# Reordering three queues where a run of seven-product blocks begins (single core, fp32 in two halves)

## The chip, the cores and the metric

One NeuronCore of a Trainium2 chip runs the whole program. The metric is the device time of one execution in microseconds (us); the kernel before took a median of 1065.38 us in 3 runs (1064.78 to 1068.34).

## The reference

The input is x, four sequences of 512 rows of 512 features, and two layers follow each other:

```python
q, k, v = x @ Wq, x @ Wk, x @ Wv
a = softmax(q @ k.T * 512**-0.5) @ v @ Wp + bp
cms = gelu(a @ cW1 + cb1) @ cW2 + cb2 + one_hot(code)        # hidden width 2048
mod = gelu(concat([a, cms]) @ mW1 + mb1) @ mW2 + mb2         # hidden width 2048
y = clip(x + cms + mod, 0, 1)
z = y + gelu(y @ W_down[s] + b_down[s]) @ W_up[s] + b_up[s]  # s: expert of the sequence, 3 experts
out = layernorm(z) * ln_w[s] + ln_b[s]
```

Everything is fp32. The kernel makes each fp32 operand into a high half (rounded to the fast matmul format, fp32r) and a low half (the rest), and each product is three matmuls: high x high, high x low, low x high.

## The kernel before

**Tiling.** After attention the kernel walks through 32 groups g. Groups 0 to 15 are the layer cms, groups 16 to 31 (`MOD0` = 16) the layer mod. A group takes 256 hidden columns of one pair of sequences. Its up-projection is a two-by-two block product made with seven products (i = 0 to 6, `product_part`) instead of eight; each has its left operand (a sum of blocks of the weights, `left_x` for the half that multiplies a, `left_c` for the half that multiplies cms) and its right operand (a sum of blocks of the activations). The seven results are joined by VectorE (`join`) into four tiles C11, C22, C21, C12, on which ScalarE applies the gelu (`gelu`), writing H_hi and an fp32 copy; VectorE then makes H_lo (`gelu_low`).

**The down-projection** of group g-1 is done by TensorE inside group g. For the groups in `FOUR` it is the plain `out_tiles`. For the groups in `SEVEN`, which are two runs, `RUNS` = groups 16 to 21 and groups 24 to 30, it is also a seven-product scheme: seven steps j = 0 to 6 (`block_step`), each with two tiles of three matmuls. Steps 0, 1 and 4 take H itself; steps 2, 3, 5 and 6 take the sums T1, T2, T3 and T4 of H (`sum_T` on VectorE, their high half by `T_hi` on ScalarE, their low half by `low_T` on VectorE). The prepared slices of the weights come through four buffers (`ring`), refilled by SyncE in `refill(g-1, j)` after step j has been done. A run begins in group 17 (steps of group 16) and in group 25 (steps of group 24).

**TensorE's order in a group of a run** is fixed: product 0, product 1, steps 0 and 1, product 2, product 3, step 2, product 4, steps 3 and 4, product 5, step 5, product 6, step 6. Step 4 waits until the results of step 2 are added (`add_step`), step 6 until those of step 5 are.

**The other engines** have handwritten orders, each in program order, joined by semaphores:

- SyncE (SP) issues nearly all DMAs: `load_left` (raw columns of the weights, rawX and rawC, 512 KB each), `load_piece` and `save_piece` (24 pieces of the adapter's weights are read, split and stored in memory as high and low halves, one piece a group, groups 3 to 26), `load_staged` (x or cms tiles that are added into acc), `refill`, and in group 24 the saving of the finished `acc` of sequences 0 and 1 and its reloading with x of sequences 2 and 3 (1 MB each, `x_in_acc`).
- GpSimd (POOL) makes the weight sums (`sums_13`, `sum_2`, `sum_4`) and all low halves of left operands (`left_lo`), of pieces (`piece_split`), in group 24 of three operands of cms (`co_lo`, 128x1024), and at the end of y (`y_lo`) and of the last plain second operand (`second_lo`).
- ScalarE (ACT) makes the high halves (`left_hi`, `T_hi`, `piece_to_hi`, `second_hi`) and the gelus. In group g, `left_hi(s, t, 0, g)` waits for the raw columns just loaded, `left_hi` 1, 2 and 4 wait for sums by POOL.
- VectorE (DVE) in a group of a run follows `seven_group`: gelu_low C21, sums V, T3, T4, add_step 0, sum T1, add_step 1, sum T2, low T1, join U2, low T3, T4, T2, add_step 2, join U3 and C22, add_step 3, gelu_low C11, add_staged, add_step 4, join C21, gelu_low C22, add_step 5, join C12, add_step 6.

Of the kernel before, what the change touches and what calls it, by code (L numbers as in the profile page):

```python
# [7 lines left out]
def layers_kernel(nc, x, xT, codes, streams, WqT, WkT, WvT, Wp, bias_cols, cW1, cW2, mW1, mW2,  # L8
# [28 lines left out]
    with ctx:  # L37
# [403 lines left out]
        def _(sp):  # L441
# [30 lines left out]
            def load_left(s, t):  # L472
                if t > 0:
                    sp.wait_ge(A_made[s], 7 * t)
                elif s == 0:
                    sp.wait_ge(WvpT_lo_made, 2 * KT - 1)
                else:
                    sp.wait_ge(out_filled, outputs(MOD0 - 3, 1, 3))
                w = cW1 if s == 0 and t < 8 else mW1[V * s:V * (s + 1), :]
                sp.dma_start(raw[s][:, :, :], w[:, 2 * P * (t % 8):2 * P * (t % 8 + 1)].rearrange("(k p) c -> p k c", p=P)).then_inc(raw_loaded[s], 16)  # L480
# [34 lines left out]
            def refill(g, *steps):  # L515
                for j in steps:
                    if (g, j) in ring_next:
                        sp.wait_ge(out_filled, step(g, j, 1))
                        for load in ring_next[g, j]:
                            load_ring(*load)  # L520
# [6 lines left out]
            def load_piece(u):  # L527
                if u > 0:
                    sp.wait_ge(piece_saved, 32 * u)
                sp.dma_start(piece_raw[:, :], adapter[u // PARTS, u % PARTS]).then_inc(piece_loaded, 16)  # L530

            def save_piece(u):
                e, part = u // PARTS, u % PARTS
                sp.wait_ge(piece_lo_made, u + 1)
                for half, tile in enumerate((piece_hi, piece_lo)):
                    sp.dma_start(experts[e, half, :, 256 * part:256 * (part + 1)], f32(tile[:, :])).then_inc(piece_saved, 16)

            def load_staged(g):
                for i in added_tile(g):
                    if i == 0:  # L540
                        sp.wait_ge(cms_saved[1], 16 * KT)
                    if i > 1:
                        sp.wait_ge(staged_added, i - 1)
                    if g - 1 in SEVEN:
                        sp.wait_ge(out_filled, step(g - 1, 2, 1))
                    elif g - 2 in SEVEN:
                        sp.wait_ge(out_filled, step(g - 2, 6, 1))
                    h, m = i // KT % 2, i % KT
                    src = xT[h, m * P:(m + 1) * P, :] if i < 8 else cms_kept[h, m]
                    sp.dma_start(staged_at(g, i), src).then_inc(staged_loaded[i % 2], 16)  # L550
# [55 lines left out]
            for g in range(MOD0, GROUPS):  # L606
                sets = splits_in(g)
                if g == MOD0:
                    load_left(*sets[0])
                    load_piece(g - 3)  # L610
                    for h in range(2):
                        for m in range(KT):
                            sp.wait_ge(summed, outputs(MOD0 - 1, h, m))
                            sp.dma_start(cms_kept[h, m], acc[:, 2 + h, m, :]).then_inc(cms_saved[h], 16)
                    load_staged(g)
                    fill_ring(g - 1)
                    load_left(*sets[1])
                    save_piece(g - 3)
                    continue
                for s, t in sets:  # L620
                    load_left(s, t)
                if g - 1 not in SEVEN:
                    load_staged(g)
                if g in PIECE_GROUPS:
                    load_piece(g - 3)
                if g - 1 in SEVEN and g < GROUPS - 1:
                    refill(g - 1, 0, 1, 2)
                    load_staged(g)
                    refill(g - 1, 3, 4)
                    if g in FOUR:  # L630
                        load_second(second_set(g))
                    refill(g - 1, 5)
                if g == 23:
                    sp.wait_ge(made, products(g, 0))
                    cms_home(0, B11, B21)
                    sp.wait_ge(made, products(g, 1))
                    cms_home(1, T3, B22)
                    for i in range(2):
                        x1_home(i)
                if g == 24:  # L640
                    sp.wait_ge(clipped, KT)
                    sp.dma_start(y_kept[0], flat(acc[:, 0])).then_inc(y_saved, 16)
                    sp.wait_ge(y_saved, 16)
                    sp.dma_start(acc[:, 0], weight(xT[2])).then_inc(x_in_acc[0], 16)
                if g == GROUPS - 1:
                    sp.wait_ge(made, products(g, 0))
                    sp.dma_start(flat(y01[0][:, :, :]), y_kept[0]).then_inc(y_back[0], 16)
                    sp.wait_ge(made, products(g, 1))
                    sp.dma_start(flat(y01[1][:, :, :]), y_kept[1]).then_inc(y_back[1], 16)
                    sp.wait_ge(piece_saved, 32 * PIECES)  # L650
                    load_adapter(0, (0, 1))
                    refill(g - 1, 0, 1, 2)
                    load_staged(g)
                    sp.wait_ge(made, products(g, 3))
                    load_adapter(0, (2, 3))
                    refill(g - 1, 3)
                    sp.wait_ge(made, products(g, 4))
                    load_adapter(1, range(4))
                    load_second(second_set(g))
                    refill(g - 1, 4, 5)  # L660
                if g in FOUR and g - 1 in FOUR:
                    load_second(second_set(g))
                if g - 1 in FOUR and g in SEVEN:
                    fill_ring(g - 1)
                if g == 24:
                    sp.wait_ge(clipped, 2 * KT)
                    sp.dma_start(y_kept[1], flat(acc[:, 1])).then_inc(y_saved, 16)
                    sp.wait_ge(y_saved, 32)
                    sp.dma_start(acc[:, 1], weight(xT[3])).then_inc(x_in_acc[1], 16)
                if g == 23:  # L670
                    for i in range(2, 7):
                        x1_home(i)
                if g in PIECE_GROUPS:
                    save_piece(g - 3)
                if g - 1 in SEVEN:
                    refill(g - 1, 6)
            sp.wait_ge(made, products(GROUPS - 1, 5))
# [27 lines left out]
        def _(pool):  # L705
# [124 lines left out]
            for g in range(GROUPS):  # L830
                for s, t in splits_in(g - 1) if g > 0 else []:
                    left_lo(s, t, 6)
                    if s == 0 and g - 1 in FOUR and g - 2 in SEVEN:
                        second_lo(second_set(g - 1))
                sets = splits_in(g)
                if g == MOD0:
                    sums_13(*sets[0])
# [54 lines left out]
                    second_lo(second_set(g))  # L892
                for s, t in sets:
                    left_lo(s, t, 5)
                if g in PIECE_GROUPS:
                    piece_split(g - 3)
                if g == GROUPS - 1:
                    for b in range(2):
                        for h in range(2):
                            pool.wait_ge(made, products(g, 2))  # L900
                            pool.wait_ge(y01_hi_made, 2 * b + h + 1)
                            lo(y_lo[b][h][:, :, :], y01[b][:, HALF * h:HALF * (h + 1), :], y_hi[b][h][:, :, :], y01_lo_made)
                if g == GROUPS - 1:
                    second_lo(second_set(g))

            for n in range(POOL_ROWS):
                b, t = n // TT, n % TT
# [251 lines left out]
        def _(act):  # L1159
# [193 lines left out]
            for g in range(GROUPS):  # L1353
# [27 lines left out]
                if g == 1:  # L1381
                    for op in (T3, T4):
                        xo_hi(1, op)
                if g - 1 in SEVEN:
                    T_hi(g - 1, "T1")
                    for s, t in sets[:1]:
                        left_hi(s, t, 0, g)
                    T_hi(g - 1, "T2")
                for i in (0, 1):
                    for s, t in sets[g - 1 in SEVEN and i == 0:]:  # L1390
                        left_hi(s, t, i, g)
                    if g == MOD0 and i == 0:
                        act.wait_ge(cms_saved[1], 16 * KT)
                        for k in (5, 6):
                            left_hi(1, 0, k)
# [5 lines left out]
                    left_hi(1, 0, 0)  # L1401
                for s, t in sets:
                    left_hi(s, t, 2, g)
                gelu(g, C11)
                if g == MOD0:
                    left_hi(*splits_in(g)[1], 0, g)
                if g == 23:
# [26 lines left out]
                if g in PIECE_GROUPS:  # L1434
                    piece_to_hi(g - 3)
            add_b_up(0)
            gelu(GROUPS - 1, C12)
            second_hi(second_set(GROUPS - 1))

            def gelu_adapter(b):  # L1440
                for m in range(BT):
# [476 lines left out]
```

## Time and profile before

| | |
|---|---|
| median of 3 runs | 1065.38 us |
| the profiled execution's own time | 1066.87 us |
| its span, first to last instruction | 1065.1 us |
| mean granted TensorE clock | 0.995 of full speed |
| PE (TensorE matmul) busy | 1051.9 us, 99% |
| DVE, ACT, POOL busy | 68%, 44%, 55% |
| DMA | 37% of 16 engines' span, 125 GB/s |

The times are those of one execution seen by the hardware profiler. Busy time of PE counts matmuls that overlap in the pipeline; how fast they follow each other is seen from their starts. A wait is put down to what was released last; "issue" means that the profile shows nothing.

### The profile page before, as it was taken

Reading aid. Unit: us, or ns where it says so; the run is one execution under the profiler, and the core shown is the slowest. Engines: PE = TensorE matmul, PEld = TensorE weight load, DVE = VectorE, ACT = ScalarE, POOL = GpSimd, SP = SyncE. Lnnn points to the kernel's source line nnn. Section 1 sums busy time; section 2 is a strip of 40 time slices with the busy share of each in tenths; the row PEclk is TensorE's granted clock in tenths of the full one; section 3 lists DMA queues with packets and bytes.
Section 4 is the critical chain, followed back from the end, with each engine's and each line's share of the span. In section 5 each row is a group of like instructions: output and inputs, shape, how many; then the busy total and the mean of one; then the engine's idle time right before and its main releaser. Section 6 shows DMA issues by size and latency. Waiting matters only on the chain. (4 is left out here: it accounts for less than half of the span.)

```text
span 1065.1 us, 13654 instructions
## 1 busy us (share of the span) xinstructions
PE 1051.9 (99%) x4675; PEld 868.9 (82%) x4675; DVE 719.4 (68%) x1020; ACT 473.0 (44%) x901; POOL 586.5 (55%) x577
## 2 busy tenths in 40 slices
PE   9999999999999999999999999999998999999998
PEld 7888888888888888888887888888886888888886
DVE  3735353396565555555786888885797888887868
ACT  3645345454334334333553443443554334343765
POOL 0565774632332331431878767777897666673406
PEclk9999999999999999999999999999999999999999
DMA  7456630101223322111053443435865433345824
GB/s 277 136 171 199 227 109 1 59 1 46 74 74 104 119 74 94 50 35 55 23 176 118 130 125 124 131 107 158 324 220 173 130 122 115 106 117 170 324 80 158
DMA packets 88212, 134.10 MB, mean 126 GB/s; under 512 B 7376, under 2 KB 53200, under 8 KB 87632
## 3 DMA queue, kind: packets, MB, share of 16 engines
q1 hardware_dynamic: 87568, 132.18, 37.2%
q10 hardware_dynamic: 576, 1.05, 0.3%
q8 instruction: 38, 0.62, 0.2%
q14 instruction: 30, 0.25, 0.1%
HBM read 98.34 MB, written 34.87 MB: 125 GB/s over the span
## 5 line engine op out<-in xcount | busy, mean ns | idle before, releaser
L714 POOL TENSOR_TENSOR left_x<-rawX,left_x 128x256 fp32r<-128x256 f32 x144 | 134.5, 935 | 150.9 <-ACT left_x L1202 150.9
L1649 DVE TENSOR_TENSOR acc<-bank,acc 128x512 f32<-128x512 f32 x136 | 92.1, 688 | 50.8 <-PE bank L919 50.3
L1708 DVE TENSOR_TENSOR acc<-bank,acc 128x512 f32<-128x512 f32 x166 | 107.0, 683 | 24.3 <-PE bank L919 22.0
L917 PE MATMUL bank<-H_hi,W_hi 128*128 128x512 f32 x304 | 118.4, 390 | 0.4 <-POOL W_lo L714 0.4
L918 PE MATMUL bank<-H_lo,W_hi 128*128 128x512 f32 x304 | 118.3, 389 | 0.0
L919 PE MATMUL bank<-H_hi,W_lo 128*128 128x512 f32 x304 | 118.3, 389 | 0.0
L917 PE MATMUL bank<-x_T_hi,left_x 128*128 128x512 f32 x256 | 99.8, 390 | 0.0
L918 PE MATMUL bank<-x_T_lo,left_x 128*128 128x512 f32 x256 | 99.8, 390 | 0.0
L919 PE MATMUL bank<-x_T_hi,left_x 128*128 128x512 f32 x256 | 99.6, 389 | 0.0
L1638 DVE TENSOR_TENSOR u_t<-bank,s_t 128x512 f32<-128x512 f32 x64 | 44.0, 688 | 75.7 <-PE bank L919 73.6
L714 POOL TENSOR_TENSOR left_c<-rawC,left_c 128x256 fp32r<-128x256 f32 x96 | 91.2, 950 | 3.8 <-ACT left_c L1202 3.8
L1202 ACT ACTIVATE left_x<-rawX 128x256 fp32r<-128x256 f32 x144 | 57.7, 408 | 63.9 <-POOL rawX L728 44.6
L714 POOL TENSOR_TENSOR piece_lo<-piece_raw,piece_hi 128x256 fp32r<-128x256 f32 x24 | 20.1, 839 | 106.0 <-ACT piece_hi L1331 106.0
L917 PE MATMUL bank<-x_B_hi,left_x 128*128 128x512 f32 x192 | 74.9, 390 | 0.0
L918 PE MATMUL bank<-x_B_lo,left_x 128*128 128x512 f32 x192 | 74.9, 390 | 0.0
L919 PE MATMUL bank<-x_B_hi,left_x 128*128 128x512 f32 x192 | 74.8, 390 | 0.0
L1315 ACT ACTIVATE H_hi<-u_t,bias 128x512 fp32r<-128x512 f32 x51 | 36.6, 717 | 86.0 <-PE bank L919 83.3
L1315 ACT ACTIVATE H_hi<-bank,bias 128x512 fp32r<-128x512 f32 x32 | 22.0, 687 | 111.0 <-PE bank L919 111.0
L917 PEld LDWEIGHTS bank<-H_hi,W_hi 128*128 128x128 f32 x304 | 57.0, 188 | 12.8 <-POOL W_lo L714 1.1
L919 PEld LDWEIGHTS bank<-H_hi,W_lo 128*128 128x128 f32 x304 | 57.1, 188 | 12.0
L918 PEld LDWEIGHTS bank<-H_lo,W_hi 128*128 128x128 f32 x304 | 57.1, 188 | 11.7
L917 PE MATMUL bank<-H_hi,ring 128*128 128x512 f32 x156 | 61.3, 393 | 2.6 <-issue 2.6
(224 smaller groups left out, 2825.7 us busy)
## 6 DMA issues: line engine op xcount, KB each, us to landing
ring<-w_kept SPq DMA_DIRECT2D x91, 256.0 KB, 2.7
rawX<-mW_dram SPq DMA_DIRECT2D x16, 512.0 KB, 4.1
rawC<-mW_dram SPq DMA_DIRECT2D x16, 512.0 KB, 4.8
w_kept<-mod_hi SPq DMA_DIRECT2D x7, 896.0 KB, 4.4
w_kept<-mod_lo SPq DMA_DIRECT2D x7, 896.0 KB, 7.2
xT_raw<-xT_dram SPq DMA_DIRECT2D x4, 1024.0 KB, 8.1
x_raw<-x_dram SPq DMA_DIRECT2D x4, 1024.0 KB, 6.3
rawX<-cW_dram SPq DMA_DIRECT2D x8, 512.0 KB, 3.7
```

Source lines behind the costliest of these rows:

```text
L714: pool.tensor_tensor(dst, src, f32(hi), ALU.subtract).then_inc(done, 1)
L917: pe.matmul(tile, sh, mh, start=first_one and n == 0, stop=False, skip_group_check=joined_group)
L918: pe.matmul(tile, sh, ml, start=False, stop=False, skip_group_check=joined_group)
L919: last = pe.matmul(tile, sl, mh, start=False, stop=last_one and n == len(terms) - 1, skip_group_check=joined_group)
L1202: act.activation(left(s, i)[0], left_source(s, i), ACT.Copy).then_inc(A_hi_made[s], 1)
L1315: act.activation(dst, src, ACT.Gelu, bias=bias[:, column:column + 1]).then_inc(gelu_made, 1)
L1638: dve.tensor_tensor(dst[:, :], bank[b][:, :], other[:, :], ALU.add).then_inc(joined, 1)
L1649: op = dve.tensor_tensor(dst, src, dst, ALU.add)
L1708: dve.tensor_tensor(dst, src, dst, ALU.add).then_inc(summed, 1)
```

## The change

All edits are orders; no operation is added or left out.

- ScalarE, groups 17 and 25 (`run_starts`): high half of T2 ahead of left operand 0 of x, and gelu of C11 directly behind left operands 0, ahead of 1 and 2.
- SyncE: a piece is stored in the next group, behind `load_left`, and the next one is loaded behind the staged tiles (in group 24 behind the ring's first slices); group 16 no longer ends with a save. x of sequence 3 is loaded into `acc` in group 25, behind the raw columns and the piece's save.
- GpSimd, groups from 17 on: a piece is split in the next group, behind left operands 6. At the end `second_lo` goes ahead of the last of four y_lo.
- ScalarE, end of group 31: `second_hi` ahead of the gelu of C12.

```diff
@@ SyncE, groups from 16 on
                     fill_ring(g - 1)
                     load_left(*sets[1])
-                    save_piece(g - 3)
                     continue
                 for s, t in sets:
                     load_left(s, t)
+                if g - 1 in PIECE_GROUPS:
+                    save_piece(g - 4)
                 if g - 1 not in SEVEN:
                     load_staged(g)
-                if g in PIECE_GROUPS:
-                    load_piece(g - 3)
                 if g - 1 in SEVEN and g < GROUPS - 1:
+                    if g == 25:
+                        sp.wait_ge(y_saved, 32)
+                        sp.dma_start(acc[:, 1], weight(xT[3])).then_inc(x_in_acc[1], 16)
                     refill(g - 1, 0, 1, 2)
                     load_staged(g)
+                    if g in PIECE_GROUPS:
+                        load_piece(g - 3)
                     refill(g - 1, 3, 4)
...
                     for i in range(2):
                         x1_home(i)
+                    load_piece(g - 3)
...
                 if g == 24:
+                    load_piece(g - 3)
                     sp.wait_ge(clipped, 2 * KT)
                     sp.dma_start(y_kept[1], flat(acc[:, 1])).then_inc(y_saved, 16)
-                    sp.wait_ge(y_saved, 32)
-                    sp.dma_start(acc[:, 1], weight(xT[3])).then_inc(x_in_acc[1], 16)
...
-                if g in PIECE_GROUPS:
-                    save_piece(g - 3)
                 if g - 1 in SEVEN:
                     refill(g - 1, 6)
@@ GpSimd
                     left_lo(s, t, 6)
                     if s == 0 and g - 1 in FOUR and g - 2 in SEVEN:
                         second_lo(second_set(g - 1))
+                if g > MOD0 and g - 1 in PIECE_GROUPS:
+                    piece_split(g - 4)
...
-                if g in PIECE_GROUPS:
+                if g < MOD0 and g in PIECE_GROUPS:
                     piece_split(g - 3)
                 if g == GROUPS - 1:
                     for b in range(2):
                         for h in range(2):
+                            if b == 1 and h == 1:
+                                second_lo(second_set(g))
                             pool.wait_ge(made, products(g, 2))
...
-                if g == GROUPS - 1:
-                    second_lo(second_set(g))
@@ ScalarE
+                run_starts = g - 1 in (RUNS[0][0], RUNS[1][0])
                 if g - 1 in SEVEN:
                     T_hi(g - 1, "T1")
-                    for s, t in sets[:1]:
+                    for s, t in sets[:0 if run_starts else 1]:
                         left_hi(s, t, 0, g)
                     T_hi(g - 1, "T2")
                 for i in (0, 1):
-                    for s, t in sets[g - 1 in SEVEN and i == 0:]:
+                    for s, t in sets[g - 1 in SEVEN and i == 0 and not run_starts:]:
                         left_hi(s, t, i, g)
+                    if run_starts and i == 0:
+                        gelu(g, C11)
...
                 for s, t in sets:
                     left_hi(s, t, 2, g)
-                gelu(g, C11)
+                if not run_starts:
+                    gelu(g, C11)
...
             add_b_up(0)
+            second_hi(second_set(GROUPS - 1))
             gelu(GROUPS - 1, C12)
-            second_hi(second_set(GROUPS - 1))
```

## Rows read from the trace of the kernel before

**Rows 1.** The waits of PE over the whole span: us in total, times, longest.

```profile
PE bank L917 <- DVE acc L1708: 3.4, 2, 3.1
PE bank L917 <- issue: 2.6, 2, 2.2
```

**Rows 2.** PE by stretches: length, busy (matmuls), clock granted, DMA share, GB/s.

```profile
573.20:588.82 15.62, 13.07 (x49) 0.89 0.44 152
606.50:617.39 10.89, 10.89 (x49) 1.00 0.32 84
809.20:828.45 19.25, 15.78 (x61) 0.91 0.39 126
```

**Rows 3.** The same view, a shorter stretch.

```profile
823.00:826.20 3.20, 3.20 (x9) 0.50 0.06 18
```

**Rows 4.** PE in order of time: start, duration, line, op, [idle before <- releaser].

```profile
575.63 0.47 PE L917 MATMUL bank<-H_hi,ring 128*128 128x512 f32 x1 [2.25 <-issue]
...
776.60 0.39 PE L917 MATMUL bank<-c_B_hi,left_c 128*128 128x512 f32 x1
...
809.78 0.47 PE L917 MATMUL bank<-H_hi,ring 128*128 128x512 f32 x1 [0.39 <-issue]
...
822.67 0.58 PE L917 MATMUL bank<-T_hi,ring 128*128 128x512 f32 x1 [3.08 <-DVE acc L1708]
...
1003.13 0.50 PE L917 MATMUL bank<-H_hi,W_hi 128*128 128x512 f32 x1 [0.43 <-POOL W_lo L714]
```

**Rows 5.** ACT in order of time, groups 17, 24 and 31.

```profile
573.59 0.42 ACT L1202 ACTIVATE left_x<-rawX 128x256 fp32r<-128x256 f32 x1 [7.43 <-DMA rawX<-mW_dram]
573.91 0.61 ACT L1319 ACTIVATE H_hi<-H_f 128x512 fp32r<-128x512 f32 x1
...
794.21 0.40 ACT L1331 ACTIVATE piece_hi<-piece_raw 128x256 fp32r<-128x256 f32 x1
...
999.55 1.06 ACT L1209 ACTIVATE W_hi<-W_raw 128x1024 fp32r<-128x1024 f32 x1 [0.51 <-DMA W_raw<-mW_dram]
```

**Rows 6.** The page's group of ACT's gelu of C11: xcount | busy, mean ns | idle.

```profile
L1315 ACT ACTIVATE H_hi<-bank,bias 128x512 fp32r<-128x512 f32 x32 | 22.0, 687 | 111.0 <-PE bank L919 111.0
```

**Rows 7.** DVE in order of time, groups 17 and 25.

```profile
574.56 0.97 DVE L1690 TENSOR_TENSOR H_lo<-H_f,H_hi 128x512 fp32r<-128x512 f32 x1 [5.06 <-ACT H_hi L1319]
...
801.84 0.68 DVE L1690 TENSOR_TENSOR H_lo<-H_f,H_hi 128x512 fp32r<-128x512 f32 x1
...
816.08 1.02 DVE L1624 TENSOR_TENSOR H_lo<-gelu_f,H_hi 128x512 fp32r<-128x512 f32 x1 [2.37 <-ACT gelu_f L1315]
...
821.84 1.28 DVE L1708 TENSOR_TENSOR acc<-bank,acc 128x512 f32<-128x512 f32 x2
```

**Rows 8.** POOL in order of time, groups 16 to 17, then 24.

```profile
566.58 1.19 POOL L714 TENSOR_TENSOR piece_lo<-piece_raw,piece_hi 128x256 fp32r<-128x256 f32 x1
...
568.92 1.18 POOL L714 TENSOR_TENSOR left_c<-rawC,left_c 128x256 fp32r<-128x256 f32 x1
...
770.84 3.39 POOL L714 TENSOR_TENSOR c_B_lo<-c_B_f,c_B_hi 128x1024 fp32r<-128x1024 f32 x1
...
798.76 0.74 POOL L714 TENSOR_TENSOR left_x<-rawX,left_x 128x256 fp32r<-128x256 f32 x1
```

**Rows 9.** SyncE's DMA issues in order of time.

```profile
571.87 1.38 SPq L513 DMA_DIRECT2D ring<-w_kept  x3
...
799.54 0.38 SPq L669 DMA_DIRECT2D acc<-xT_dram  x1
```

**Rows 10.** DMA issues: KB each, median us to landing; page, 569.5 to 574, 799 to 802.

```profile
ring<-w_kept SPq DMA_DIRECT2D x91, 256.0 KB, 2.7
...
ring<-w_kept SPq DMA_DIRECT2D x3, 256.0 KB, 4.4
...
acc<-xT_dram SPq DMA_DIRECT2D x1, 1024.0 KB, 5.9
rawC<-mW_dram SPq DMA_DIRECT2D x1, 512.0 KB, 7.6
```

## The prediction

> **What bounds the kernel now.** The page's first part, in the table above, has PE busy for 99% of the span, so nothing is gained but by closing PE's own gaps. The list of PE's waits is the next view: over the whole span it stands for 3.4 us on adds by VectorE and 2.6 us on "issue" [rows 1], and little else. Then PE by stretches. From step 3 of group 18 to its end TensorE is undisturbed: 48 matmuls (the view's 49 counts one cut by the edge) in 10.89 us, 0.227 us each, at the full clock. The same 48 matmuls in group 17 take 15.62 us; in group 25 the same work and the 12 matmuls of the next product take 19.25 us where 60/48 x 10.89 = 13.61 would do [rows 2]. So the start of the first run loses 15.62 - 10.89 = 4.73 us, that of the second 19.25 - 13.61 = 5.64 us, together 10.37 us. That is more than the waits, because the granted clock falls too: 0.89 and 0.91 as means of the stretches, 0.50 (1.2 GHz of 2.4) inside the second, right behind its stop [rows 2, 3]. About 1.6 us of each loss is this half clock: 3.4 us of it at half speed, from 1.00 - 0.89 = 0.11 of 15.62 us taken twice.
>
> PE in order of time gives the places [rows 4]. I call a product 12 x 0.227 = 2.72 us and a step 6 x 0.227 = 1.36 us.
> - 575.63, group 17, step 3, after 2.25 us of idle: its operand is T2.
> - 809.78, group 25, step 3 again, 0.39 us.
> - 822.67, group 25, step 6, 3.08 us, for the adds of step 5.
> - 1003.13, the last group's plain tiles, 0.43 us, for POOL's W_lo.
>
> **Why T2 is late.** ACT stood 7.43 us before left operand 0 at 573.59, for the raw columns; T2's high half came only behind it, at 573.91, and VectorE, which had been idle for 5.06 us, made the low half from 574.56 to 575.53 [rows 5, 7]. PE went on at 575.63. T2's sum is ahead of all that in VectorE's order, so T2 was ready for ACT before 569.50, when VectorE's idle time began.
>
> **Why the adds of step 5 are late.** VectorE's chain from gelu_low of C11 is gelu_low, staged adds, add_step 4, join C21, gelu_low C22, add_step 5. In group 25 it begins at 816.08, after 2.37 us of waiting for ACT's gelu, and its first add of step 5 ends at 821.84 + 0.64 = 822.48: 6.4 us [rows 7]. The gelu itself stands in ACT's order behind left operands 2, whose sums POOL starts only when the raw columns are there.
>
> **Edit 1, T2 first (ACT).** In group 17 its high half is made before 569.5, its low half by 569.50 + 0.97 = 570.5; PE asks at 573.2. In group 25, where VectorE's T1 low half was at 801.84 [rows 7], three more operations of 0.6 us separate it from T2's: about 804.9 against 809.2. Both stops at step 3 go. Next in line is step 4.
>
> **Edit 2, C11's gelu early (ACT).** It still needs the results of step 3. In group 25 PE does that from 809.2 to 810.6; +0.15 for the pipeline, two activations of 0.69 us [rows 6] give 812.1, and the chain's 6.4 us give 818.5. PE, running through, reaches step 6 at 809.2 + 3 x 1.36 + 2 x 2.72 = 818.7. So it just fits, by 0.2 us, and I keep 0 to 0.8 us of stop, taking 0.2. In group 17 the chain has one staged tile instead of two and about 1.2 us more of room. ACT now stands before the gelu with left operands 1 behind it. POOL waits for those until about 812.4 in group 25, but PE wants them in group 26, at 820.1 + 2.7 = 822.8: nothing is lost.
>
> The 6.4 us hold one size that can move. Low halves on VectorE take 0.68 us at 801.84 and 1.02 us at 816.08 for the same shape [rows 7]. The Trainium skill's page "SBUF — State Buffer", section Who interferes with whom, says that a VectorE instruction with two SBUF inputs and a GpSimd instruction that reads SBUF share a port pair, and the later one blocks. By that rule the chain would be up to 1 us shorter if POOL stood still while it ran, and the 0.2 us would go; but POOL, released by left operands 1, runs again from 812.4, so I leave the chain as measured.
>
> **Edit 3, pieces split and stored behind left 6 (POOL, SP), group 17.** Before, POOL split the piece at 566.58 for 1.19 us ahead of left 6, whose second half ran 568.92 to 570.10 [rows 8]. Now the left operands end at about 567.8 and 568.9, so the raw loads go 1.2 to 1.9 us earlier; the split ends at 570.1 as before. SP then issues two stores (an issue costs 0.46 us, from 1.38 for 3 [rows 9]) and the ring's slices for steps 4, 5 and 6 at 571.0, against 571.87. Loading the next piece, with its wait, is out of the way. Slice 4 is wanted at 573.2 + 1.36 = 574.6. A ring load takes 2.7 us as the median of 91 and 4.4 us in this very place, behind the raw columns and the piece [rows 10]: landing at 573.7 to 575.4. The raw loads are now 2 to 3 us ahead of it, not 1.7, so I take 574.4: no stop, but up to 0.8 us stays in the range; I take 0.2. In the later groups of the runs SP waits for the split before it asks for slices 4 to 6. These have cover: from the end of step 0, when slice 4 may be asked for, to step 4 there are 2 x 1.36 + 1.36 + 3 x 2.72 = 12.2 us, less 2.7 for the load. The piece load behind the staged tiles has 5 us or more there; nothing for either.
>
> **Edit 4, x of sequence 3 in group 25 (SP).** It was issued at 799.54 and took 5.9 us [rows 9, 10]; rawX and rawC stood behind it, and rawC took 7.6 us. Now they go first, which is what feeds POOL and ACT. The price is that the add of step 2 gets its x later. POOL's left 6 was at 798.76 [rows 8]. It gains 1.2 us by the split behind it and loses 0.7 to 1.7 us by the previous piece's split, which now stands in front of the three `co_lo` of group 24, so its second half ends at about 800.5 and the split at 801.5. Two stores, then x at 802.5 to 803.3; +5.9 gives 808.4 to 809.2, +7.6 (behind the raw columns) 810.1 to 810.9. Step 4 starts at 810.6 and waits for the first add of step 2, 0.64 us: x must be there by 809.9. I take 808.8, so nothing, and keep 0 to 1 us. The first `co_lo`, moved by 0.7 to 1.7 us, ended at 770.84 + 3.39 = 774.23 and PE needs it at 776.60 [rows 4, 8]: covered; beyond 2.4 us it would cost one for one.
>
> The page "DMA: Bandwidth & Descriptors" of the Trainium skill, section Queues, rings and completion order, says that each engine takes the descriptors of one issuing queue in ring order. Taken strictly, x would wait for every byte of the raw columns, which is the 7.6 us end, and the sum would be about 0.6 us smaller; the trace's 4.4 against 2.7 us for a ring slice agrees.
>
> **Edit 5, piece 21 behind the ring's slices in group 24 (SP).** ACT took it at 794.21 [rows 5]. It is now issued around 789.6, ahead only of the saving of sequence 1, whose landing released SP at 799.54 [rows 9]; that save is 1 MB, some 3 us of transfer, so the piece lands at 796 to 797.5. ACT, and with it C12's gelu, T3, the adds and T1, come 2 to 3.3 us later. T1's low half ended at 802.52 and PE asks at 809.2 - 2.72 - 1.36 = 805.1: room for 2.6 us. 0 to 0.8 us; I take 0.2.
>
> **Edit 6, second_lo and second_hi at the end.** ACT began W_hi at 999.55, released by the DMA, and POOL's W_lo followed it at once: neither stood behind what it is moved past [rows 4, 5]. Worth nothing; the 0.43 us stay. C12's gelu and the last y_lo, 2 to 2.5 us later, are used after a further 5.4 us of matmuls.
>
> **Sum.** 10.37 us less 0.2 (step 6), 0.2 (slice 4), 0.2 (T1) = 9.8 us. 1066.87 - 9.8 = 1057.1 us for an execution like the profiled one; the median is 1.49 us below that one, so 1055.6 us.
>
> **Rivals.**
> - *x arrives late.* Step 4 of group 25 stands for the add of step 2. It decides if x lands after 809.9; the row of rawC speaks for it, the one of x itself against. A stop of 1 us shifts the whole chain to step 6 as well, which has 0.2 us; with the half clock (1.6 us) 2.6 to 3.5 us come back: 1058.5 us. Chance 0.15.
> - *Slice 4 arrives late in group 17.* 0.8 us, and the clock perhaps falls again: 2.4 us back, 1058.0 us. Against it: the two short stops of 0.39 and 0.43 us [rows 4] had no fall of the clock behind them. 0.12.
> - *The second chain doesn't close.* ACT's gelu of C11 waits for something else, or POOL slows VectorE: the 3.08 us of step 6 shrink to 1.5 only and the clock still falls, so 1.5 + 1.6 = 3.1 us come back: 1058.7 us; if the first start fails in the same way, 1061.8 us. 0.10.
> - *Slower.* SP is one queue, and in each of the nine groups of the runs that have a piece to store it now waits for POOL's split before it fetches slices 4 to 6. This decides once POOL's left 6 and split end more than 9.5 us (12.2 - 2.7) after step 0; PE arrives some 5 us earlier at groups 18 and 26 than before, POOL only 2 to 3 us. If it bites by 1 us with the half clock in most of them, 8 x 2.6 = 21 us are added and 9.8 gained: 1077 us. PE has no wait at all in groups 18 to 22 now (the list [rows 1] is of the whole span), and POOL's 55% leave it time to catch up. 0.03.
>
> The forecast has 0.60. **Range:** the low end is the sum with no residue and a median 1 us luckier, 1053.8 us; the high end takes in the first three rivals' usual size, 1060.3 us. A change within 0.3% (3.2 us, about what a measurement of this kernel can tell from none) would need two thirds of the gain to fail. Faster 0.91, same 0.06, slower 0.03.
>
> **What would show it.** Right: PE's list without "issue"; step 3 of groups 17 and 25 joined to product 4; ACT's T2 near 569 and 804; gelu of C11 at 574.7 and 810.8; the stretches of rows 2 near 10.9 and 13.6 us with clock 1.00; W_lo's 0.4 us still there. Wrong: a stop before step 4 in either group, released by the ring or by an add of step 2; T1 late in group 25; a half clock without a long stop; a wait of SP for the split that reaches PE.

## The result, and the profile after

| | before | after |
|---|---|---|
| median, 6 runs each | 1067.2 us | 1061.5 us (1059.8 to 1062.52) |
| ratio, 95% interval | | 0.9944 [0.9929, 0.9959] |
| profiled span | 1065.1 us | 1060.7 us |
| PE's stops from 210 us on, sum | 11.0 us | 6.95 us |

Faster, by 5.7 us of 1067.2, where 9.8 was forecast; 1061.5 us lies above the range of 1053.8 to 1060.3. The three runs on which the forecast's level rested were 1.8 us faster than the median of six (1065.38 against 1067.2), which would put the forecast at 1057.4 us. The other 4.1 us are gain that did not come. The profiled execution after took 1062.52 us and is the slowest of its six, so its stops may be about 1 us more than those of a middle one.

"Stops" here and below: two matmuls in a row start 0.227 us apart at full speed, and what a pair has beyond that is lost. It is read from the starts in PE's order of time and is 0.1 to 0.2 us more than the idle time printed there. Each stop at full clock costs a further 0.08 to 0.11 us one matmul later. At half clock the excess of every matmul counts.

PE's list of waits of the kernel after (us in total, times, longest), to set beside [rows 1]:

```profile
PE bank L921 <- DVE acc L1716: 1.8, 2, 1.0
PE bank L947 <- POOL ident L712: 1.5, 1, 1.5
PE bank L921 <- DMA ring<-w_kept: 1.4, 1, 1.4
PE bank L921 <- POOL W_lo L716: 1.4, 1, 1.4
PE bank L921 <- issue: 0.7, 1, 0.7
```

The longest stop is 1.4 us instead of 3.1, but there are five of them. (POOL's ident is at the start of the program and is in every kernel.) The stretches of [rows 2], from step 3 to the end of step 6, with the next product in the second:

```profile
572.78:586.36 13.58, 11.45 (x50) 8.85 (x48) 10.21 (x14) 7.95 (x19) 12.06 (x16) 1.00 0.51 166
808.04:823.12 15.08, 14.05 (x62) 11.11 (x60) 14.43 (x20) 8.55 (x20) 13.84 (x17) 1.00 0.43 142
```

The columns are length, busy (count) of PE, weight loads, VectorE, ScalarE and GpSimd, then clock, DMA share, GB/s. Group 17 went from 15.62 to 13.58 us where 10.89 was wanted, group 25 from 19.25 to 15.08 where 13.61 was. The clock is 1.00 in both: the half clock is gone. PE in order of time gives the five places:

```profile
575.67 0.50 PE L921 MATMUL bank<-H_hi,ring 128*128 128x512 f32 x1 [1.37 <-DMA ring<-w_kept]
...
584.89 0.47 PE L921 MATMUL bank<-T_hi,ring 128*128 128x512 f32 x1 [0.77 <-DVE acc L1716]
...
803.86 0.47 PE L921 MATMUL bank<-H_hi,ring 128*128 128x512 f32 x1 [0.75 <-issue]
...
818.91 0.47 PE L921 MATMUL bank<-T_hi,ring 128*128 128x512 f32 x1 [1.03 <-DVE acc L1716]
...
998.71 0.50 PE L921 MATMUL bank<-H_hi,W_hi 128*128 128x512 f32 x1 [1.35 <-POOL W_lo L716]
```

They are step 4 of group 17 (1.53 us by the starts), its step 6 (0.93), step 2 of group 25 (0.91), its step 6 (1.19) and the last group's plain tiles (1.51). None is at step 3, where T2 held PE before. The mean granted clock is 0.999 or 1.0 in all six executions, so it was not this one alone that lost the half clock. Each has its own cause, and the other engines' order of time shows it.

**Step 4 of group 17: slice 4.** SyncE's issues, and the issues with their median time to landing:

```profile
567.34 0.38 SPq L480 DMA_DIRECT2D rawX<-mW_dram  x1
568.54 0.84 SPq L480 DMA_DIRECT2D rawC<-mW_dram  x1
...
570.57 1.47 SPq L513 DMA_DIRECT2D ring<-w_kept  x3
```
```profile
ring<-w_kept SPq DMA_DIRECT2D x3, 256.0 KB, 5.2
rawX<-mW_dram SPq DMA_DIRECT2D x1, 512.0 KB, 3.9
rawC<-mW_dram SPq DMA_DIRECT2D x1, 512.0 KB, 5.7
```

Everything was asked for earlier than before (slice 4 at 570.57 against 571.87 [rows 9]) and took longer (5.2 us against 4.4 [rows 10]): slice 4 came at 575.62, wanted at 574.1. By the semaphore's events in the trace it came in 16 parts, from 574.14 to 575.62, and PE went on behind the last of them, at 575.67; in the kernel before they came from 575.69 to 576.06. The spread of 1.5 us is about as long as the stop. Fifteen parts were there by 575.09; why the last one lagged no run shows.

**Step 6 of group 17: the gelu of C22.** ScalarE and VectorE:

```profile
575.20 0.68 ACT L1319 ACTIVATE gelu_f<-bank,bias 128x512 f32<-128x512 f32 x1
...
579.49 0.42 ACT L1206 ACTIVATE left_c<-rawC 128x256 fp32r<-128x256 f32 x1 [1.43 <-POOL rawC L730]
...
581.66 0.71 ACT L1319 ACTIVATE H_hi<-u_t,bias 128x512 fp32r<-128x512 f32 x1
...
583.01 1.13 DVE L1632 TENSOR_TENSOR H_lo<-u_t,H_hi 128x512 fp32r<-128x512 f32 x1 [2.24 <-ACT u_t L1319]
584.07 1.27 DVE L1716 TENSOR_TENSOR acc<-bank,acc 128x512 f32<-128x512 f32 x2
```

Left operand 1 of the half that multiplies cms (left_c) waits for a sum by POOL that was ready at 579.4. Seven high halves, this one included, go before the gelu of C22 in ScalarE's order, the low half of C22 behind that gelu, and the adds of step 5 behind the low half. PE had stood at this step in the kernel before too, for 0.31 us (0.47 by the starts), the second of the two waits in [rows 1]:

```profile
587.36 0.47 PE L917 MATMUL bank<-T_hi,ring 128*128 128x512 f32 x1 [0.31 <-DVE acc L1708]
```

**Step 2 of group 25: piece 21.** ACT stood for the piece until 796.00, and T1's low half started at 802.54:

```profile
796.00 0.42 ACT L1335 ACTIVATE piece_hi<-piece_raw 128x256 fp32r<-128x256 f32 x1 [4.17 <-DMA piece_raw<-adapter_dram]
```
```profile
802.54 1.22 DVE L1698 TENSOR_TENSOR H_lo<-H_f,H_hi 128x512 fp32r<-128x512 f32 x1
```

**Step 6 of group 25: x.** VectorE, and the DMA issues of 800 to 802.6:

```profile
808.55 1.41 DVE L1714 SCALAR_TENSOR_TENSOR acc<-bank,bias,acc 128x512 f32<-128x512 f32 x2 [1.85 <-DMA acc<-xT_dram]
...
812.59 0.74 DVE L1632 TENSOR_TENSOR H_lo<-gelu_f,H_hi 128x512 fp32r<-128x512 f32 x1
```
```profile
acc<-xT_dram SPq DMA_DIRECT2D x1, 1024.0 KB, 7.3
```

C11's gelu was done at 810.95 (two activations from 809.68), its low half began only at 812.59. In between VectorE did what the late x had held up: the add of step 2, two joins, the add of step 3. That is 1.6 us, and the stop at step 6 is 1.19.

**The end: W_raw.** ScalarE and GpSimd in group 31:

```profile
995.15 1.06 ACT L1213 ACTIVATE W_hi<-W_raw 128x1024 fp32r<-128x1024 f32 x1 [2.67 <-DMA W_raw<-mW_dram]
```
```profile
996.29 2.37 POOL L716 TENSOR_TENSOR W_lo<-W_raw,W_hi 128x1024 fp32r<-128x1024 f32 x1 [3.69 <-ACT W_hi L1213]
```

W_raw took 9.9 us to land, and both of its users stood waiting for it.

### The profile page after: what moved, and what is told of

It is laid out like the page before. It is cut to its first block, busy times and chain, and to the rows that moved or that the text cites. A ratio compares the mean times of both kernels' runs of the same rounds, so it can differ in the third digit from the quotient of the medians.

```text
span 1060.7 us, 13654 instructions
## 1 busy us (share of the span) xinstructions
PE 1048.7 (99%) x4675; PEld 866.4 (82%) x4675; DVE 721.6 (68%) x1020; ACT 473.5 (45%) x901; POOL 591.9 (56%) x577
## 4 chain that ended last, share of the span: by engine, by line
PE 87%; POOL 4%; DVE 3%; DMA 3%; issue 2%; ACT 1%; SPq 0%; DVEq 0%; ACTq 0%; POOLq 0%
PE bank L921 28%; PE bank L923 28%; PE bank L922 28%; POOL left_c L716 1%; POOL left_x L716 1%; DMA piece_raw<-adapter_dram 1%; DVE c_T_f L1580 1%; DMA acc<-xT_dram 1%; PE bank L978 1%; PE bank L1144 1%; DVE acc L1657 0%; DVE acc L1724 0%; DMA ring<-w_kept 0%; POOL rawC L730 0%; DVE H_lo L1632 0%
## 5 line engine op out<-in xcount | busy, mean ns | idle before, releaser
L716 POOL TENSOR_TENSOR piece_lo<-piece_raw,piece_hi 128x256 fp32r<-128x256 f32 x24 | 23.8, 992 | 106.1 <-ACT piece_hi L1335 106.1
```

What stands on the lines that cost most here:

```text
L716: pool.tensor_tensor(dst, src, f32(hi), ALU.subtract).then_inc(done, 1)
```

## Experiments

Theory A reads the five stops as above: ScalarE's order (the third sum behind left operands 1) and four transfers. The ratio is to runs of the kernel before on the same chip, whose median was 1067.15 us (15 runs) for ring17, piece21, end_undone and act_only, 1067.6 (17) for c22, w_raw, sp_pool_only and best, and 1066.38 (7) for x_back and act_c22_wraw. Stops are given in the order step 4 and step 6 of group 17, step 2 and step 6 of group 25, W_lo; the sum holds the small ones too. The kernel after: 1.53, 0.93, 0.91, 1.19, 1.51, sum 6.95 us. Stops are those of one profiled execution, the times medians of 4 to 10.

**ring17: slices 4 and 5 ahead of the raw columns in group 17.**

```diff
+                if g in (17,):
+                    refill(g - 1, 0, 1)
                 for s, t in sets:
                     load_left(s, t)
...
-                    refill(g - 1, 0, 1, 2)
+                    refill(g - 1, *((2,) if g in (17,) else (0, 1, 2)))
```

> The changed kernel with one more move: in group 17 SyncE asks for the ring's slices for steps 4 and 5 ahead of the raw columns, in an idle stretch. Theory A (landings): the stop of 1.53 us ahead of step 4 is slice 4 standing in the DMA queue behind 1 MB of raw columns and a piece, so it goes, and PE waits there for nothing; the time falls by 1 to 1.6 us against the changed kernel, ratio to before about 0.993. The stop of 0.9 us before step 6 of group 17 stays or grows by up to 1 us, for the gelu of C22 hangs on rawC, which still lands near 574.2. Theory B (order of the engines: ACT's gelu of C11 ahead of left operands 1 makes the stops): slice 4 is only the first in line, PE stops at step 4 or 5 for a result of VectorE and the sum of the two stops, 2.5 us, stays.

Measured 1062.41 us, 0.9963 [0.995, 0.9976], span 1060.0. Stops: none, 2.04, 1.30, 1.34, 0.98, sum 6.07. The stop of slice 4 is gone and that of step 6 has grown by 1.11 us: they are in series, and the second is set by ScalarE and GpSimd, who did not move:

```profile
581.47 0.71 ACT L1321 ACTIVATE H_hi<-u_t,bias 128x512 fp32r<-128x512 f32 x1
```

581.47 against 581.66. By the interval this is no better than the kernel after: the removal of one stop in a series was worth nothing. Four of the ten executions have a mean granted clock of 0.996 to 0.998 and are the four slowest (1063.48 to 1066.29 us); the other six, at 0.999 or 1.0, took 1060.68 to 1062.98 us, about what the kernel after takes. With a stop of about 2 us the clock seems to fall in some executions and not in others; the profiled one is of the second kind, and where it fell in the four no trace shows.

**c22: C22's gelu ahead of left operands 1 as well.**

```diff
                     if run_starts and i == 0:
                         gelu(g, C11)
+                        gelu(g, C22)
...
-                gelu(g, C22)
+                if not run_starts:
+                    gelu(g, C22)
```

> The changed kernel with the gelu of C22 also ahead of left operands 1 in groups 17 and 25. In the changed kernel ACT stood before left operand 1 of c until 579.5, for POOL's third sum, and the gelu of C22 came at 581.7, its low half at 583.0. Theory A (that place in ACT's order makes the stop before step 6 of group 17): it goes, 0.9 us. In group 25 the stop of 1.2 us stays, for there VectorE is late by x of sequence 3. Time 1 us under the changed kernel. Theory B (the staged tile, which landed at 577.6, sets it): the stop stays at 0.5 us or more.

Measured 1060.31 us, 0.9924 [0.9895, 0.9953]. Stops: 1.80, none, 1.41, 1.16, 1.43, sum 6.61. The stop of group 17's step 6 is gone, that of group 25 is not (x holds it), and ScalarE shows why:

```profile
577.67 0.72 ACT L1319 ACTIVATE H_hi<-u_t,bias 128x512 fp32r<-128x512 f32 x1 [1.54 <-PE bank L923]
```

The gelu now waits for PE itself and is 4 us earlier.

**piece21: the piece loaded behind the save of piece 20**, at the head of group 24's loads, instead of behind the ring's slices.

```diff
                 if g - 1 in PIECE_GROUPS:
                     save_piece(g - 4)
+                if g == 24:
+                    load_piece(g - 3)
...
                 if g == 24:
-                    load_piece(g - 3)
                     sp.wait_ge(clipped, 2 * KT)
```

> The changed kernel with piece 21 loaded behind the store of piece 20 again, ahead of the saving of y in group 24, so that it is there long before ACT asks. Theory A: ACT's idle time of 4.2 us in front of it goes, T1's low half is 2 us earlier, PE's stops of 0.14 and 0.91 us before product 3 and step 2 of group 25 go. POOL's left 6 and the raw columns are then 2 us earlier too, and x of sequence 3 with them, so the 1.2 us before step 6 shrink to 0.5 or less. Time 1 to 2 us under the changed kernel. Theory B: T1 stays late because the adds of VectorE are what it waits for; stop of about 0.9 us stays before step 2, and the time is the same.

Measured 1060.43 us, 0.9947 [0.993, 0.9964], span 1057.7. Stops: 0.50, 0.80, none, 1.11, 1.41, sum 4.52. Step 2's stop is gone, alone of the five. The stop at step 6 was expected to shrink to 0.5 us or less, and did not: x landed 2.8 us earlier, at 805.60, but PE was 2.8 us earlier too. That of slice 4 shrank as well, by 1.0 us, with nothing changed in group 17; more on that below.

**x_back: edit 4 alone undone**, x asked for in group 24 again, ahead of the raw columns.

```diff
-                    if g == 25:
-                        sp.wait_ge(y_saved, 32)
-                        sp.dma_start(acc[:, 1], weight(xT[3])).then_inc(x_in_acc[1], 16)
...
                     sp.dma_start(y_kept[1], flat(acc[:, 1])).then_inc(y_saved, 16)
+                    sp.wait_ge(y_saved, 32)
+                    sp.dma_start(acc[:, 1], weight(xT[3])).then_inc(x_in_acc[1], 16)
```

> The changed kernel with edit 4 alone undone: x of sequence 3 is asked for behind the saving of sequence 1 in group 24 again, ahead of the raw columns of group 25. Theory A (the stop of 1.19 us at step 6 of group 25 is x's landing at 808.43, which holds VectorE's add of step 2 and all behind it): x lands by 804, gelu_low of C11 starts within 0.2 us of its gelu, and the stop at step 6 shrinks to 0.6 or less; the raw columns land 1 to 2 us later without a stop of their own; step 4 of group 17, step 6 of group 17, step 2 of group 25 and W_lo keep 0.9 to 1.9 us each. Median 1060.3 to 1061.2 us. Rival B (the raw columns' later landing moves the stop: gelu of C22 waits behind left operands 1 instead, as in the run with ScalarE's edits alone): the stop at step 6 keeps 0.9 to 1.3 us and the time stays at 1061.5. Rival C (x did not matter): as after in every stop.

Measured 1058.88 us, 0.9928 [0.99, 0.9956], span 1057.1. Stops: 1.03, 0.71, 0.36 (with 0.30 two products earlier), none, 0.95, sum 3.90. x and the raw columns, by issue and landing:

```profile
797.48 0.38 SPq L672 DMA_DIRECT2D acc<-xT_dram  x1
```
```profile
acc<-xT_dram SPq DMA_DIRECT2D x1, 1024.0 KB, 5.6
rawX<-mW_dram SPq DMA_DIRECT2D x1, 512.0 KB, 6.7
rawC<-mW_dram SPq DMA_DIRECT2D x1, 512.0 KB, 7.6
```

x came at 803.1 instead of 808.4 and the stop at step 6 went; rawC came at 806.1 instead of 805.0; ScalarE stood 1.16 us for it, PE did not. Edit 4 cost its own stop, 1.2 us. Rival B fell: C22's gelu stood behind left operands 1, at 813.13, in time. Step 2 of group 25 and step 6 of group 17 were expected to keep 0.9 us or more and came out at 0.36 and 0.71; nothing in their orders had moved.

**w_raw: the second operand's load ahead of the adapter's in group 31.**

```diff
-                    load_adapter(1, range(4))
                     load_second(second_set(g))
+                    load_adapter(1, range(4))
```

> The changed kernel with the last raw operand W_raw asked for ahead of the four 512 KB loads of adapter 1, after step 4. Theory A (the 1.5 us stop before the last plain tiles is its landing, behind 2 MB in the queue): it lands 4 us earlier or more, W_lo is made before the 24 matmuls with y are over, and the stop is gone: 1.5 us under the changed kernel. Only now the moved second_lo is worth something. Theory B (ACT's or POOL's place for it): the stop stays near 1 us.

Measured 1060.71 us, 0.9925 [0.9899, 0.9951], span 1057.9. Stops: 0.61, 0.83, 1.39, 1.33, none, sum 4.78. W_raw took 5.9 us instead of 9.9 and the last stop is gone.

**end_undone: edit 6 alone undone** (`second_lo` behind the fourth y_lo, `second_hi` behind the gelu of C12).

```diff
-                            if b == 1 and h == 1:
-                                second_lo(second_set(g))
...
+                if g == GROUPS - 1:
+                    second_lo(second_set(g))
...
-            second_hi(second_set(GROUPS - 1))
             gelu(GROUPS - 1, C12)
+            second_hi(second_set(GROUPS - 1))
```

> The changed kernel with the end of group 31 as before: second_hi behind the gelu of C12 and second_lo behind all four y_lo. Theory A: the stop before the last plain tiles, 1.5 us against 0.6 before, is the landing of W_raw (9.9 us instead of 8.5), so it stays at 0.6 to 1.5 us and the time is that of the changed kernel within 0.5 us. Theory B: the two moved operations lengthen it, and it is back at 0.6 us.

Measured 1062.19 us, 0.9956 [0.994, 0.9973]. Stops: 1.42, 0.47, 1.23 (and 0.48), 1.34, 1.86, sum 7.43. GpSimd began W_lo at 996.22, after 1.71 us of waiting for W_hi, against 996.29 with edit 6. Edit 6 moves nothing while W_raw is late. The stop of 1.86 us lies above the 0.6 to 1.5 that were expected: W_raw took 10.2 us.

**act_only: the kernel before with ScalarE's edits of groups 17 and 25, and no others.** The diff is that of ScalarE's queue without its last hunk.

> The kernel before with the edit on ScalarE alone (T2 and gelu of C11 ahead in groups 17 and 25), nothing of SyncE and POOL moved. Theory A: it is the larger part of the gain. Group 17: the stop at step 3 goes, but slice 4 was asked for at 571.87 and lands at 576.1, so PE stops 1.5 us before step 4 in its place. Group 25: step 3's 0.4 us go; slice 4 is issued at 806.6 and lands at 810.2, in time; x of sequence 3 is in time, gelu of C11 starts at 810.8, but rawC lands at 809.2 and left 1 and the gelu of C22 wait for POOL's third sum, so step 6 stops 1 to 2 us instead of 3.1. About 4 to 5 us gained, ratio 0.9955. Theory B: the order on ScalarE alone gives most of the changed kernel's remaining stops and no more than 2 us.

Measured 1061.0 us (1060.64 to 1061.47), 0.995 [0.9933, 0.9966], span 1058.8. Stops: 1.00, 1.25, none, 1.08, 1.18, sum 5.02. That is the gain of the whole change: on top of these two edits, all the others together move neither median nor interval. Slice 4 cost 1.0 us of the 1.5 expected; the 1.25 us at step 6 of group 17 were not expected. At step 6 of group 25 x is in time (5.9 us to landing, from 797.36), and the trace has C22's gelu behind left operands 1 there too (act_c22_wraw below tests it):

```profile
812.22 0.42 ACT L1202 ACTIVATE left_c<-rawC 128x256 fp32r<-128x256 f32 x1 [1.87 <-POOL rawC L728]
...
814.39 0.71 ACT L1315 ACTIVATE H_hi<-u_t,bias 128x512 fp32r<-128x512 f32 x1
```

**sp_pool_only: the change without these edits of ScalarE.**

```diff
-                run_starts = g - 1 in (RUNS[0][0], RUNS[1][0])
+                run_starts = False
```

> The changed kernel without its edits on ScalarE in groups 17 and 25: only SyncE's, POOL's and the end's moves are left. Theory A (the edits on ScalarE give the gain, those on SyncE and POOL only move transfers): T2 waits again for rawX, which now lands 1.9 us earlier in group 17 and 5 us earlier in group 25, so step 3 stops about 0.5 us in group 17 and not at all in 25; step 4 stops 1 to 1.5 us for slice 4; gelu of C11 is late again, and step 6 stops 0.5 us in group 17 and up to 2 us in 25; T1 of group 25 is late by piece 21 as in the changed kernel. About 2 to 4 us gained on the kernel before, ratio 0.997. Theory B (the raw columns' earlier loading is what gains): 0.995 as the changed kernel, and ScalarE's edits add nothing to it.

Measured 1064.07 us, 0.9959 [0.9942, 0.9977], span 1063.9. Stops: 0.58, 2.29, 1.28, 1.30, 1.33, and 0.69 at step 3 of group 17, 0.35 at product 3 of group 25; with a half clock the sum is 10.2. So the moves of SyncE and GpSimd do gain by themselves, 3.5 us between the medians, but at the same stops as ScalarE's: step 3 of group 17 went from 2.41 to 0.69 and step 6 of group 25 from 3.24 to 1.30 us. The two gains overlap and don't add. Loading the raw columns earlier does bring T2's high half forward, to 571.83 from 573.91 [rows 5]. The stop at step 6 of group 17 grew from 0.47 us to 2.29, and behind it the clock fell. This profiled execution, 1065.69 us, is the slowest of ten (the fastest took 1062.29), so its sum stands high.

```profile
586.22 0.47 PE L921 MATMUL bank<-T_hi,ring 128*128 128x512 f32 x1 [2.13 <-DVE acc L1716]
```
```profile
586.60:590.00 3.40, 3.40 (x10) 2.62 (x9) 2.60 (x5) 1.89 (x5) 3.08 (x6) 0.50 0.03 8
```

**act_c22_wraw: the kernel before with ScalarE's edits of groups 17 and 25, c22 and w_raw**, and none of the moves of SyncE and GpSimd.

> The kernel before with three moves and none of SyncE's and GpSimd's edits of the change: ScalarE's edits of groups 17 and 25 (T2's high half first, gelu of C11 behind left operands 0), the gelu of C22 also ahead of left operands 1 there, and in group 31 the second operand's raw load ahead of the adapter's. Theory A (each stop is ScalarE's order or a landing, and the moved loads and stores of the change bring nothing): of the 5.02 us of stops in the run with ScalarE's edits alone, both stops at step 6 (1.25 and 1.08) and that of W_lo (1.18) go, step 4 of group 17 keeps 0.5 to 1.5 us; sum about 1.3 us, median 1056.5 to 1057.8 us, and no half clock. Rival B (in group 25 x, issued ahead of the raw columns, and VectorE's order hold step 6 by themselves): the stop at step 6 of group 25 stays near 1 us, 1057.8 to 1058.8. Rival C (SyncE's and GpSimd's edits are what lets the chain close): both stops at step 6 stay, 1059.5 or more.

Measured 1058.15 us (1057.67 to 1058.44, 4 runs), 0.9923 [0.9895, 0.9951], span 1056.3. Stops: 2.19, none, none, none, 0.60, sum 3.29. Both chains close without edits 3 to 5, so rival C fell, and with x ahead of the raw columns, so B did. Two expectations missed: slice 4 cost 2.19 us, not 0.5 to 1.5, and W_lo kept 0.60 us. For W_lo, GpSimd and ScalarE show a cause:

```profile
983.92 7.60 POOL L714 TENSOR_TENSOR y_lo<-y,y_hi 128x1024 fp32r<-128x1024 f32 x3
991.46 2.86 POOL L714 TENSOR_TENSOR W_lo<-W_raw,W_hi 128x1024 fp32r<-128x1024 f32 x1
```

W_hi was made from 990.17 to 991.23, and here POOL had no idle time ahead of W_lo: with the load early, the orders that edit 6 changes are next in line. In w_raw, where edit 6 is in, the stop is gone; no run undoes edit 6 alone there.

**best: all repairs together** on the changed kernel: slices 4 and 5 ahead of the raw columns in groups 17 and 25, piece21, x_back, c22 and w_raw.

> All repairs together: the changed kernel with slices 4 and 5 of the ring ahead of the raw columns in groups 17 and 25, piece 21 loaded before the saving of y, x of sequence 3 in its old place ahead of the raw columns, the gelu of C22 ahead of left operands 1, and W_raw ahead of adapter 1. Theory A: every stop has one of these causes, so all of the changed kernel's 6.2 us of stops go but some 0.5 us: ratio to before 0.989 to 0.990, 1055 us. Theory B (a limit of VectorE's chain and of DMA bandwidth stands behind them): new stops of 2 us or more take their place, 0.992.

Measured 1055.71 us (1054.97 to 1056.15, 4 runs), 0.9873 [0.9832, 0.9915], span 1054.0. No stop is left but 0.31 us of small ones. PE's whole list, and the same stretches:

```profile
PE bank L949 <- POOL ident L714: 1.5, 1, 1.5
```
```profile
573.14:584.02 10.88, 10.88 (x49) 9.01 (x48) 9.55 (x14) 8.12 (x19) 10.40 (x13) 1.00 0.41 136
804.43:818.13 13.70, 13.70 (x62) 11.19 (x60) 13.37 (x18) 9.46 (x22) 13.70 (x17) 1.00 0.51 169
```

These are the 10.89 and 13.61 us that the prediction took as the floor, the second within 0.1 us. Whether edits 3 and 5 are needed for it is not tested: act_c22_wraw does without them, and 2.8 of its 3.29 us of stops are slice 4's and W_lo's.

## Why the prediction was wrong

**What held.** Edit 1: T2's high half was ready before 569.5 and both stops at step 3 are gone. Edit 2: the gelu of C11 came at 574.63 and 809.68 (said: 574.7, 810.8; PE was 1.2 us earlier at step 3 of group 25 than the prediction reckoned). The chain behind it took 6.1 us in group 25, from 812.59 to 818.73 (said: 6.4). The half clock went with the long stops. act_only shows that these two edits suffice for the whole gain; sp_pool_only shows that the others alone would have brought 3.5 us of it at the same stops. Edit 6 was worth nothing, as said. The slower rival did not come: the list has no wait behind a split in the later groups of the runs.

**The number.** From the same three runs the range's high end, 1060.3, stands for a gain of 5.1 us, and 5.7 came. So the time fell outside the range by the level of before, 1.8 us, and by the missing 4.1 us together; either alone would have left it inside.

**What failed.** The sum left 0.6 us of residue beside the 0.59 at the end of before; the trace has 6.95. Point by point, forecast against the stop:

- *Slice 4, 0.2 us taken, 1.53 measured.* Edit 3 bounded the landing with 2.7 and 4.4 us of before and took 574.4, a flight of 3.4 us, because raw loads asked for earlier would be out of the way. Asked for at 570.57, 1.3 us earlier than before, it flew 5.1 us, beyond both bounds, its parts spread (elsewhere in before's trace a slice took 5.2 us, at 545.3, and 7.9 us, at 789.1); and PE wanted it at 574.1, not 574.6. ring17 shows that it is this transfer: ahead of the raw columns, no stop. Without edit 3 the stop was 1.00 and 2.19 us (act_only, act_c22_wraw), so these runs do not show that edit 3 did anything for slice 4. This rival had 0.12 at 0.8 us.
- *Step 6 of group 17, nothing taken, 0.93 measured.* Edit 2 followed the chain from the gelu of C11 and gave group 17 1.2 us of room more. It passed over the 0.31 us that PE stood at this very step before, though [rows 1] counts two waits for VectorE and its list of places has one. The chain as listed holds gelu_low of C22, but not what that waits for: C22's gelu still stood behind left operands 1, which the same step had seen wait for POOL; "nothing is lost" was asked only of PE's use of left 1. Shown by c22: that gelu came 4 us earlier and the stop went. The rival "the second chain doesn't close" had the place but not this cause, and priced it at 3.1 us with a half clock that did not come.
- *Piece 21, 0.2 us taken, 0.91 measured.* Edit 5's landing (796 to 797.5) was met at 796.0, with two errors against each other: asked for at 787.87, not 789.6, it flew 8.1 us. The room of 2.6 us was wrong, because it was read in the time of before: PE came to step 2 of group 25 at 802.96, not 805.1, mostly since group 17 had given back 2.0 us (15.62 - 13.58). piece21 shows that the piece is the cause.
- *x, nothing taken, 1.19 measured.* The landing (808.8) was right, 808.4, but by luck: x was asked for at 801.10 instead of 802.5 to 803.3 and flew 7.3 us instead of 5.9. The step that failed was the test "x must be there by 809.9", taken from the one consumer on PE, step 4. That test was in before's time too: PE began step 4 at 809.45, so x had to be there by about 808.7, and it was, by 0.3 us. VectorE's queue is in order, and x held its head from 806.7. The next joins and gelu_low of C11 came 1.6 us late, and the harm appeared at step 6. The rival "x arrives late" named step 6 as well, but only for an x after 809.9, with a stop at step 4 first; step 4 had none. x_back shows that x is the cause.
- *The end, 0.43 us kept, 1.35 idle measured.* It was taken as a constant, though it is a DMA landing: 9.9 us where before's was 8.5. w_raw shows that the landing is the cause. It took 9.4 to 10.3 us in every other run with this order of loads, in act_only too, where no load was moved. So it was not the moved transfers that made it longer than before's 8.5 us; what did is not shown.

Four of the five are landings or rooms read from before's time, though the edits moved PE and most of the transfers. Where the same order ran several times, the stop of slice 4 was 1.53, 0.50, 1.42, 1.80, 0.61 and 1.03 us (after, piece21, end_undone, c22, w_raw, x_back); one profile gives such a stop only to within a range of 1.3 us. The landing itself went from 3.8 to 5.2 us. That scatter also bounds what single differences in the sums mean: the repairs are shown by a stop that vanishes, not by a sum that falls by 1 us.

## What to carry to other kernels

When an edit lets the bounding engine run earlier, redo every later due time in its new time, and give every transfer that is asked for in a burst the longest landing that the whole trace has for its size in a burst, not the median and not that of one place. A late operand must be followed through each in-order queue that it heads: look for the last thing behind it, not for its own reader. And when several waits are in series, test the repairs together: ring17 alone gained nothing, all of them together took 11.9 us off the kernel before (1067.6 to 1055.71), twice what the change did.

## What the runs showed of the hardware

- A 256 KB slice lands in 2.7 us at the median [rows 10] and took 5.2 us as the median of three asked for after 1.25 MB of other loads and stores within 3.3 us; slice 4 took 3.8 to 5.2 us there in seven runs with this order. The 1 MB load of x took 5.5 to 5.9 us at the head of such a burst (before, act_only, act_c22_wraw, x_back, best) and 7.2 to 8.1 us behind 1.25 MB (after and the six runs that keep its place). The page "DMA: Bandwidth & Descriptors" of the Trainium skill, section Queues, rings and completion order, has each engine take one queue's descriptors in ring order; these runs agree, and moving a load ahead of the burst (ring17) or of the large loads in it (x_back, w_raw) was each time the cure.
- Behind stops of 2.41, 3.24 (before) and 2.29 us (sp_pool_only) the granted clock was 0.50 for 3.4 us; behind stops of 2.19 (act_c22_wraw), 2.04 (ring17) and all shorter ones in the profiled executions it stayed at 1.00. What of a stop decides it, these runs do not show.
